# Queries kept 8 columns apart: contiguous planes for their transfer, a strided stationary operand for the scores

## What is computed

```python
q = (x @ Wq + bq).reshape(B, S, H, hd).transpose(0, 2, 1, 3)    # H = 16, hd = 8
k = (x @ Wk + bk).reshape(B, S, H, hd).transpose(0, 2, 1, 3)
scores = jnp.einsum('bhqd,bhkd->bhqk', q, k) * scale
allowed = (j <= i) & (i - j < WINDOW)                           # WINDOW = 32
attn = jax.nn.softmax(jnp.where(allowed, scores, NEG_INF), axis=-1)
out = jnp.einsum('bhqk,bhkd->bhqd', attn, v)
```

## Time and profile before

| | us |
|---|---|
| median of 3 runs | 133.46 |
| lowest, highest | 132.75, 134.13 |
| the profiled execution's own time | 132.78 |
| its span, first to last instruction | 131.1 |
| PE, PEld, DVE, ACT, POOL busy | 100.8, 78.0, 81.4, 67.0, 68.2 |
| mean granted TensorE clock | 0.909 |

### The profile page before, as it was taken

The page is one execution under the profiler, slowest core; times in us unless marked ns, Lnnn a source line. Parts: engine busy times, 40 slices in busy tenths (PEclk is TensorE's granted clock), DMA queues, the critical chain, the costliest instruction groups (busy, mean ns, idle before and its releaser), DMA issues.

```text
span 131.1 us, 4518 instructions
## 1 busy us (share of the span) xinstructions
PE 100.8 (77%) x1885; PEld 78.0 (60%) x1885; DVE 81.4 (62%) x202; ACT 67.0 (51%) x142; POOL 68.2 (52%) x82
## 2 busy tenths in 40 slices
PE   1188985499986575978796844937979899999991
PEld 0075963488773474867675743925335477694990
DVE  2886929578789559769999799692223636101031
ACT  3222067297791757497784955586025450706100
POOL 7643806949564857447199995796003990000000
PEclk9999999955999968999999998555699999999999
DMA  3790024233133221222332423000000000202022
GB/s 105 213 283 0 0 63 62 56 58 77 30 45 70 44 41 53 39 42 59 49 56 57 60 63 45 3 5 0 0 5 0 5 0 0 80 0 80 5 80 80
DMA packets 24435, 6.60 MB, mean 50 GB/s; under 512 B 16855, under 2 KB 24286, under 8 KB 24414
## 3 DMA queue, kind: packets, MB, share of 16 engines
q1 hardware_dynamic: 23982, 6.10, 21.3%
q10 hardware_dynamic: 432, 0.20, 0.6%
HBM read 3.15 MB, written 2.23 MB: 41 GB/s over the span
## 4 chain that ended last, share of the span: by engine, by line
PE 43%; DVE 16%; DMA 14%; SPq 10%; issue 6%; POOL 5%; ACT 3%; DVEq 0%; ACTq 0%
PE bank_s L429 11%; DMA v_scr<-v_sb 7%; PE bank_p L442 5%; SPq L182 5%; PE bank_s L338 5%; SPq L190 5%; DMA QS<-qT 5%; PE bank_t L442 4%; DVE probsT L642 4%; PE bank_o L378 4%; PE bank_o L361 3%; POOL V L261 2%; DVE rowmax L636 2%; DMA x_sb<-in_L_attn_x_dram 2%; DVE stats L611 2%
## 5 line engine op out<-in xcount | busy, mean ns | idle before, releaser
L208 POOL TENSOR_TENSOR sraw<-sraw,rowmax 128x512 f32<-128x512 f32 x32 | 32.6, 1044 | 20.5 <-DVE rowmax L636 20.5
L539 ACT ACTIVATE probs<-sraw 128x512 f32<-128x512 f32 x32 | 20.1, 641 | 12.8 <-POOL sraw L208 12.3
L636 DVE TENSOR_REDUCE rowmax<-sraw 128x8 f32<-128x512 f32 x32 | 20.4, 679 | 6.0 <-ACT sraw L505 6.0
L642 DVE STREAM_TRANSPOSE probsT<-probs 128x512 f32<-128x512 f32 x32 | 20.9, 689 | 4.3 <-ACT probs L539 4.2
L338 PE MATMUL bank_s<-KT,QS 32*128 32x64 f32 x512 | 18.1, 294 | 5.2 <-DMA QS<-qT 4.7
L338 PEld LDWEIGHTS bank_s<-KT,QS 32*128 32x128 f32 x512 | 17.6, 210 | 6.6 <-DMA QS<-qT 5.6
L557 ACT ACTIVATE hidden<-bank_s,bias_cols 128x512 f32<-128x512 f32 x16 | 11.0, 688 | 19.2 <-PE bank_s L429 19.0
L505 ACT ACTIVATE sraw<-bank_s 128x512 f32<-128x512 f32 x32 | 17.6, 613 | 5.5 <-PE bank_s L338 5.5
L361 PEld LDWEIGHTS bank_o<-V,probsT 128*32 128x32 f32 x1016 | 12.4, 123 | 7.9 <-issue 7.7
L361 PE MATMUL bank_o<-V,probsT 128*32 128x36 f32 x1016 | 13.9, 215 | 3.2 <-issue 3.2
L429 PE MATMUL bank_s<-x2T,w1T 128*128 128x512 f32 x32 | 15.0, 601 | 0.8 <-issue 0.8
(11 more groups left out here) (95 smaller groups left out, 155.6 us busy)
## 6 DMA issues: line engine op xcount, KB each, us to landing
v_scr<-v_sb SPq DMA_DIRECT2D x8, 144.0 KB, 3.1
V<-v_scr SPq DMA_DIRECT2D x32, 36.0 KB, 2.2
QS<-qT SPq DMA_DIRECT2D x28, 32.0 KB, 1.9
x_sb<-in_L_attn_x_dram SPq DMA_DIRECT2D x1, 768.0 KB, 5.2
out_dram<-y SPq DMA_DIRECT2D x3, 256.0 KB, 2.2
w<-in_L_ffn_W_dram SPq DMA_DIRECT2D x2, 256.0 KB, 5.3
x_sb<-in_L_attn_x_dram SPq DMA_DIRECT2D x2, 128.0 KB, 2.7
out_dram<-y SPq DMA_DIRECT2D x2, 128.0 KB, 1.8
```

Source lines behind the costliest of these rows:

```text
L208: nc.gpsimd.tensor_tensor(sraw[g][:], sraw[g][:], rowmax[g][:].unsqueeze(2).to_broadcast([P, BLOCKS, 2 * WIN]), ALU.subtract).then_inc(cen ...
L539: nc.scalar.activation(probs[g][:], sraw[g][:].rearrange("p j k -> p (j k)"), ACT.Exp, scale=float(HD) ** -0.5).then_inc(probs_done, 1)
L636: nc.vector.tensor_reduce(rowmax[g][:], sraw[g][:], AX.X, ALU.max).then_inc(max_done, 1)
L642: nc.vector.transpose(probsT[u % 8][:].rearrange("p j q -> p (j q)"), probs[g][:]).then_inc(probsT_done, 1)
```

## The change

QS is stored as [head plane, query, block], and qT as [query, block]. A plane of a chunk's queries is then 256 numbers in a row (1 KB) in both tiles, so each of the four DMAs copies one run per partition. The 128 columns of one block's stationary operand then stand 8 numbers (32 bytes) apart. ACT's copy to qT and VectorE's `spread_q0` write their result at that step of 32 bytes. The number and the order of the instructions on every engine stay as they were, waits included; line numbers behind L183 move up by one.

```diff
-        qT = ring(2, "qT", [P, CHUNK])
-        QS = ring(3, "QS", [P, BLOCKS, GH, WIN])
+        qT = ring(2, "qT", [P, WIN, BLOCKS])
+        QS = ring(3, "QS", [P, GH, WIN, BLOCKS])
...
                     for h in range(GH):
-                        sp.dma_start(QS[c % 3][h::GH, :, h],
-                                     qT[c % 2][h::GH].rearrange("p (j q) -> p j q", q=WIN)).then_inc(QS_in[c % 3], 16)
+                        sp.dma_start(QS[c % 3][h::GH, h], qT[c % 2][h::GH]).then_inc(QS_in[c % 3], 16)
...
-                                              QS[c % 3][rows, j].rearrange("p h q -> p (h q)"), KT[rows, k0:k0 + 2 * WIN],
+                                              QS[c % 3][rows].rearrange("p h q j -> p (h q) j")[:, :, j], KT[rows, k0:k0 + 2 * WIN],
...
-                    ident_act(qT[c % 2][:], bank_p[:, 0:CHUNK], bias=bqc).then_inc(qT_done, 1)
+                    ident_act(qT[c % 2][:].rearrange("p q j -> p j q"),
+                              bank_p[:, 0:CHUNK].rearrange("p (j q) -> p j q", q=WIN), bias=bqc).then_inc(qT_done, 1)
...
-                    nc.vector.tensor_scalar(QS[0][:, :, h], bank_o[1][:, 0:CHUNK].rearrange("p (j q) -> p j q", q=WIN),
+                    nc.vector.tensor_scalar(QS[0][:, h].rearrange("p q j -> p j q"), bank_o[1][:, 0:CHUNK].rearrange("p (j q) -> p j q", q=WIN),
                                             bqc, head_of[:, h:h + 1], ALU.add, ALU.mult).then_inc(QS_done, 1)
```

## The result

| | before | after |
|---|---|---|
| median of 6 runs each | 133.56 us | 142.81 us |
| ratio to before, 95% interval | | 1.067 (1.061 to 1.074) |
| span of the profiled execution | 131.1 us | 139.9 us |

The medians differ by 9.3 us, and the ratio says 6.7%. All ratios, here and in the experiments, leave out on both sides the runs that lay over 1.5% above the fastest of their kernel. I had forecast slower, by 3.4 us; the time lies in the stated range and far above the forecast's own (135.2 to 139).

The account below looks back on a forecast made before the run. On the 131.1 us chain, QS issue, QS landing and scores' matmuls held 5% each. Slower loads +3.9 us, less 0.5 for stalls, gave +3.4: 136.2 profiled, 136.9 us median; own range 135.2 to 139, stated range 131.9 to 147.0.

Parts of the forecast that it names:

- The loads slow down: Scores' matmuls on TensorE: loading stationary columns 32 bytes apart takes longer and lengthens each chunk's block; forecast B, chance 0.40.
- The size of this term: Scores' loads: 0.056 us of each 0.11 us step, doubled, adds 0.056 us times 16, so +0.9 us per chunk.
- about double: Factor for a load at 32 bytes, from ScalarE's copies: 0.33 us start to start for wq, 0.15 us for contiguous v_sb.
- The account chunk by chunk: Longer scores blocks cost time only where ACT waited for them: chunks 0, 2, 4, 5 +0.9 each, 6 -0.2, 7 +0.5; 3.9 us.
- The transfers: QS DMAs: issue 0.35 us shorter each, landing 1.8 instead of 1.9 us at best; quicker transfers alone give 0.5 to 1.5 us.
- Rival D: SP's queue is the real pace: all three PE waits for QS count, -4.7 us, 128.8 us; chance 0.06.
- The writes: ACT's seven qT copies and DVE's four chunk 0 planes at 32 bytes: taken as 0, up to +0.6 us if qT writes lose.
- list of signs of being wrong: Scores blocks of 2.0 us or above 4 us, a qT copy well above 0.47 us, or QS DMAs still taking 0.6 us.
- The stalls: Two PE stalls of 1.51 and 1.66 us, probably waits for instructions: a slower PE gives them time, 0.5 us set against the loss.
- Rival C: Scores' loads: each number costs what four cost now, load 0.22 us, +2.7 us per chunk, 146 us (149 at +3.4); chance 0.27.

Follow-up runs that it names:

- e1: Kernel before, with only the scores' 128 stationary columns read at a step of 32 bytes from the unchanged QS: 142.85 us, ratio 1.062 (1.053 to 1.070).
- e4: Kernel before, with 32 instead of 64 keys in each scores matmul, loads contiguous: block of 64 matmuls 1.87 us (before 1.90); single run 136.03 us.
- e7: Kernel before, with scores loads at a step of 32 bytes and 32 instead of 64 keys per matmul: blocks at full clock 3.78 to 3.81 us.
- e8: Kernel before, with 64 instead of 128 stationary columns in each scores matmul, loads contiguous: block of 64 matmuls 1.16 us (before 1.90).
- e9: Kernel before, with scores loads at a step of 32 bytes in chunks 1 and 3 alone: ratio 1.010 (1.004 to 1.017).
- e10: Kernel before, with scores loads at a step of 32 bytes in chunks 4 and 5 alone: ratio 1.033 (1.027 to 1.039).
- e2: Kernel before, with QS stored plane by plane so each DMA copies one 1 KB run per partition, writes and loads contiguous: ratio 1.002 (0.997 to 1.008).
- e3: Kernel before, with only ScalarE's copy to qT and VectorE's chunk 0 planes written at a step of 32 bytes: 135.31 us, ratio 0.997 (0.991 to 1.003).
- e5: Kernel before, with the scores' stationary columns read at a step of 16 bytes: block 3.75 us (before 1.90), 141.18 to 144.31 us in four runs.
- e6: Kernel before, with the scores' stationary columns read at a step of 8 bytes: block 2.00 us (before 1.90), 133.84 us once, 136.22 to 136.69 in three runs.

## Why the prediction was wrong in size and right in kind

- **The loads slow down, and this sets the result: right.** e1 alone gives the whole loss, within the intervals.
- **The size of this term: wrong, and this is the step that failed.** I split the step of 0.11 us between the row group's matmuls into 0.054 us of matmul and 0.056 us of load, "follow one another". The trace of before allowed the other reading, that the load lasts 0.109 us and the matmul runs beside it; e4, e7 and e8 show that one. Both readings fit one shape; two operand lengths would have been needed, and the trace has only one at L338. The load went from 0.109 to 0.228 us; doubling 0.109 over 16 steps gives +1.7 us per chunk, and +1.9 was measured, where I had +0.9. That the factor is 2.1, near my "about double", is luck. It came from another engine, and from a comparison that wasn't clean: ScalarE reads wq from SBUF, but its "contiguous" copies to v_sb read `bank_t`, which is PSUM. On TensorE the factor is the quotient of two different limits, and at half clock it is only about 1.1 (4.09 to 3.69 us).
- **The account chunk by chunk: right in the main.** With +1.9 in place of +0.9 (and +0.4 in chunk 0, from 3.67 to 4.04), the same lines give 0.4 + 0 + 1.9 + 0 + 1.9 + 1.9 + 0.8 + 1.5 = 8.4, less 0.5: 7.9 us. The span grew by 8.8. By chunk it said 1.9, 0, 1.9, 1.9, 0.8, 1.5 for chunks 2 to 7, and ACT's rows gave 1.28, 0.61, 2.01, 2.95, 0.40, 1.59: single chunks are off by up to 1.05 us, and part of this cancels. Chunk 1 was covered as forecast, but not by a start 1.9 us sooner: PE began 0.84 us sooner (23.98), and the block grew by 1.5. The distinction on which the account rests is borne out by chunk 3 of e9 and chunks 4 and 5 of e10.
- **The clock: not in the sum.** It can explain part of chunk 5's 2.95 us; see below.
- **The transfers: wrong in the issue, right in being small.** I took 0.35 us for an issue, and it stayed at 0.594; the number of runs hardly enters. The landing fell from 1.9 to 1.8 us as forecast, in e2 too. The total gain is nothing that e2 can see. What the 4.7 us of waiting for QS are worth stays open, since no run took them away with all else as before. Rival D, SP's queue as the pace, is open for the same reason: it asked for issues of 0.25 us, and these never came.
- **The writes: counted at nothing, and e3 finds nothing,** though each takes 0.18 to 0.25 us longer. The slower copy to qT and the issue of 0.6 us were on my list of signs of being wrong; neither of them made the loss.
- **The stalls: right in direction.** Of the two of 1.51 and 1.66 us, the second is down to 0.62 us in the changed kernel and the first stayed (1.60). A third, of 0.53 us inside chunk 5's block, is gone. I had not counted it. That these were waits for instructions isn't shown by any run.
- **Rival C had the mechanism:** as far as the four steps show it, each number at a step of 32 bytes needs an access of its own. The Trainium skill's rule ("Advanced Engine Details and Errata", section SBUF Cachelines) says where the penalty begins, and e5 and e6 agree with it: two numbers in each 16-byte piece cost 0.1 us per block, one number 1.85 us. What C had wrong is the price: it made the load four times as long, since it took the contiguous load to be bound by its accesses. That one follows the array's clock (blocks of 1.90 us at the full level, 3.69 at half). It touches 32 pieces, at 1.78 ns some 0.06 us of its 0.109 (an estimate). That C's 1.8 ns for an access meets the 1.78 of e1 is luck too: C worked it out from 0.44 ns per number, and so from the split that failed; the contiguous load takes 0.85 ns per number. C's sums also have slips: it takes 2.5 us for two stalls that make 3.2, and with +3.4 per chunk its own lines give 151 rather than 149.

## What to carry to other kernels

Before a layout is changed for a DMA's sake, look at who else reads it: these transfers cost no time that e2 could see, while the loads set the length of the scores. An fp32 stationary operand wants at least two numbers from each 16 bytes. Small matmuls in four row groups (here up to 64 keys) are set by their loads, so stationary columns count there and keys don't. And more work on one engine costs what the next engine behind it has no slack for: 1.9 us more in chunk 3 cost nothing, 3.9 us more in chunks 4 and 5 cost 4.5.

## What the runs showed beside this

**A load's price hardly follows the clock once it is strided.** The scores by stretch, PE and PEld busy, then the granted clock: chunks 1 and 3 of the changed kernel, then chunks 1 and 4 of e2, whose loads are contiguous.

```profile
23.90:28.10 4.20, 4.09 (x64) 3.90 (x64) 0.50 0.35 69
43.80:47.80 4.00, 3.82 (x64) 3.78 (x64) 1.00 0.16 20
```

```profile
25.20:28.95 3.75, 3.69 (x64) 3.50 (x64) 0.50 0.25 53
55.50:57.60 2.10, 1.90 (x64) 1.84 (x64) 1.00 0.33 46
```

**The granted clock was lower.** The pages' rows of the TensorE clock in 40 slices, before and after:

```profile
PEclk9999999955999968999999998555699999999999
```

```profile
PEclk9999996559959959955999959868569999999999
```

Seven slices (of 3.3 us) at 6 or below became eleven (of 3.5 us), though PE was busy 84% of the span instead of 77%. These are one trace each. Over all runs the mean granted clock was 0.808 to 0.867 in the six of the changed kernel, and 0.846 to 0.948 in the 38 of the kernel before that the experiments were measured against. One fall is seen in this table of the changed kernel, by stretch: its length, then PE, PEld, DVE, ACT and POOL busy, the clock, the DMA share and GB/s.

```profile
55.33:59.43 4.10, 4.10 (x62) 3.72 (x60) 2.03 (x6) 1.09 (x3) 1.17 (x3) 1.00 0.20 38
59.43:66.25 6.82, 6.78 (x161) 5.88 (x158) 4.26 (x9) 4.92 (x11) 3.93 (x4) 0.50 0.15 39
66.25:71.10 4.85, 4.85 (x73) 4.42 (x72) 2.70 (x7) 1.61 (x4) 0.16 (x1) 1.00 0.23 47
```

PE was never idle in the first stretch; it ran chunk 4's strided block from 56.62. Then the clock stood at half for 6.8 us, in which the rest of iteration 3 and the projections of the next ran. That the strided blocks cause the falls is not shown. PE was busy for 4.1 us ahead of this one, but idle for 1.60 us ahead of that (to 55.17). At the falls near 38.9 and 49.2, behind chunks 2 and 3, it was idle itself, for 0.70 and 1.44 us. The kernel before has such idle times too (1.51 us to 52.57) and no fall behind that one. No run tested it by itself. Nor is it settled why VectorE's copy reads at the same step without loss seen, what sets the 0.6 us of a QS issue, or what quicker transfers would be worth.
